# The last six blocks' up-projections by Strassen's seven block products, with weight sums made by GpSimd

## What is computed

```python
def _L1_cond_ref(x, t_emb, router_W, router_bias, w1, w3, w2, W1e, W2e):
    ...
    shared = jax.nn.silu(xf @ w1) * (xf @ w3) @ w2
    s = jax.nn.sigmoid((jnp.concatenate([xf, tf], axis=-1) @ router_W).astype(jnp.float32))
    ...
    h = jax.nn.gelu(jnp.einsum('nc,ech->enh', xf, W1e), approximate=False)
    y = jnp.einsum('enh,ehc->enc', h, W2e)
    routed = jnp.einsum('ne,enc->nc', combine, y)
    return ((shared + routed) / (N_SHARED + K)).reshape(Bb, Tt, C)
```

## Time and profile before

| | us |
|---|---|
| median of 3 runs (range) | 1062.59 (1060.21 to 1063.48) |
| the profiled execution: its time | 1061.99 |
| the profiled execution: its span | 1060.3 |
| PE busy | 1047.2 (99%) |
| DVE busy | 500.5 (47%) |
| ACT busy | 380.1 (36%) |
| POOL busy | 144.9 (14%) |

### The profile page before, as it was taken

The page is one execution under the profiler, slowest core; times in us unless marked ns, Lnnn a source line. Parts: engine busy times, 40 slices in busy tenths (PEclk is TensorE's granted clock), DMA queues, the critical chain, the costliest instruction groups (busy, mean ns, idle before and its releaser), DMA issues.

```text
span 1060.3 us, 15124 instructions
## 1 busy us (share of the span) xinstructions
PE 1047.2 (99%) x5098; PEld 855.1 (81%) x5098; DVE 500.5 (47%) x1054; ACT 380.1 (36%) x655; POOL 144.9 (14%) x171
## 2 busy tenths in 40 slices
PE   8999999999999999999999999999999999999998
PEld 6677777887888888888888888788888888888887
DVE  3117646456235665566555663454434244342335
ACT  3213334331226665666566663312121121211211
POOL 2020465420000000000000000322200202003020
PEclk9999999999999999999999999999999999999999
DMA  9956796997326868886577654637303333033131
GB/s 317 381 210 171 248 352 245 292 292 233 84 47 196 263 208 228 247 268 207 162 198 230 200 160 119 199 120 235 113 11 79 119 79 119 0 79 119 40 119 40
DMA packets 149416, 186.20 MB, mean 176 GB/s; under 512 B 9262, under 2 KB 93230, under 8 KB 149350
## 3 DMA queue, kind: packets, MB, share of 16 engines
q1 hardware_dynamic: 138598, 151.13, 47.4%
q0 software_dynamic: 10784, 34.61, 9.8%
HBM read 118.09 MB, written 67.63 MB: 175 GB/s over the span
## 4 chain that ended last, share of the span: by engine, by line
PE 95%; DMA 2%; DVE 2%; issue 1%; ACT 0%; SPq 0%; ACTq 0%; DVEq 0%
PE K L1573 11%; PE K L1574 11%; PE K L1575 11%; PE M L1573 5%; PE M L1574 5%; PE L L1574 5%; PE Rb L1574 5%; PE M L1575 5%; PE Rb L1573 5%; PE L L1573 5%; PE Rb L1575 5%; PE L L1575 5%; PE M L1615 2%; PE M L1617 2%; PE M L1619 2%; PE Rb L1689 2%
## 5 line engine op out<-in xcount | busy, mean ns | idle before, releaser
L505 ACT ACTIVATE slf<-K 128x512 f32<-128x512 f32 x64 | 38.2, 598 | 204.6 <-PE K L1575 204.6
L510 ACT CAST gTh<-slf 128x512 fp32r<-128x512 f32 x64 | 39.8, 621 | 182.1 <-DVE slf L520 180.5
L1573 PE MATMUL M<-w2h,gTh 128*128 128x512 f32 x256 | 99.8, 390 | 0.5 <-DVE gTl L524 0.5
L1574 PE MATMUL M<-w2l,gTh 128*128 128x512 f32 x256 | 99.6, 389 | 0.0
L1575 PE MATMUL M<-w2h,gTl 128*128 128x512 f32 x256 | 99.6, 389 | 0.0
L844 POOL DMA_INDIRECT yb<-ys_d,pos_fix x64 | 61.8, 965 | 272.5 <-DVE total L1492 254.6
L1573 PE MATMUL K<-x1h,w13h 128*128 128x512 f32 x224 | 87.2, 389 | 1.5 <-ACT yo L999 1.5
L1575 PE MATMUL K<-x1h,w13l 128*128 128x512 f32 x224 | 87.1, 389 | 0.0
L1574 PE MATMUL K<-x1l,w13h 128*128 128x512 f32 x224 | 87.1, 389 | 0.0
L520 DVE TENSOR_TENSOR slf<-L,slf 128x512 f32<-128x512 f32 x32 | 22.1, 690 | 132.7 <-PE L L1575 128.1
L1419 DVE TENSOR_TENSOR e2l<-e2raw,e2h 128x512 fp32r<-128x512 f32 x64 | 41.3, 686 | 79.9 <-ACT e2h L978 79.9
(11 more groups left out here) (298 smaller groups left out, 2475.1 us busy)
## 6 DMA issues: line engine op xcount, KB each, us to landing
w2c<-in_L_cond_w_dram SPq DMA_DIRECT2D x8, 2048.0 KB, 11.5
e1raw<-in_L_cond_W1e_dram SPq DMA_DIRECT2D x16, 1024.0 KB, 7.1
e2raw<-in_L_cond_W2e_dram SPq DMA_DIRECT2D x16, 1024.0 KB, 5.5
xr<-xs_d SPq DMA_DIRECT2D x64, 256.0 KB, 4.6
ys_d<-yo SPq DMA_DIRECT2D x32, 512.0 KB, 7.4
x_d<-x1tok SPq DMA_DIRECT2D x9, 1024.0 KB, 6.1
xs_d<-zeros SPq DMA_DIRECT2D x8, 1024.0 KB, 8.4
xres<-x_d SPq DMA_DIRECT2D x8, 1024.0 KB, 5.8
```

Of the source, the lines that this page charges most:

```text
L505: nc.scalar.activation(slf[:, h % 2], U[h % 2][:], ACT.Silu).then_inc(ffn.silu, 1)
L510: nc.scalar.copy(gTh[:, h % 2], slf[:, h % 2]).then_inc(ffn.g_hi, 1)
L1573: mm(o, ah, bh_, start=start, stop=False)
L1574: mm(o, ah, bl_, start=False, stop=False)
```

## The change

Split the 512 channels into two halves A and B, and the 512 tokens of a block into two halves. For a chunk of 128 hidden columns, (w1, w3) by (A, B) is a 2 x 2 arrangement of blocks, and the tokens are another: eight block products of 128 hidden columns by 256 channels by 256 tokens. Strassen's scheme (in Winograd's form) makes seven products of sums and differences of blocks instead. In the last six blocks of tokens the 24 matmuls of 512 columns of a chunk become 7 x 2 x 3 = 42 matmuls of 256 columns.

What this needs:

- **Weights.** For each of the 8 chunks seven weight blocks (four loaded, three of them made, plus one sum that is only a step), each cut in high and low: `wide`, 1792 + 1792 elements in each partition. POOL makes them before its first gather, for all 8 chunks in turn. Six chunks of them go out to DRAM (`wide_d`) and are loaded again in every block by transfers issued on ACT (`load_wide`, 128x3584 float32, 1.8 MB); two chunks stay in SBUF. PE and DVE begin the six blocks only when POOL is through (`WIDE_DONE`).
- **Tokens.** Four mixes of 128x512 on DVE for each block (`mix_x`), and seven casts and seven cuts (`cut_x1`) instead of four.
- **Products.** Each of the seven lands in half a bank (`place`). DVE joins them into U and V: seven additions of 128x256 for a chunk (`mix`), each with one input in PSUM, most waiting for the one before. ACT copies the first product to `m1s`. Silu now reads SBUF, in place, and the multiplication has both inputs in SBUF.
- **Order.** The silu, multiplication and cuts of a chunk stand behind the products of the next one; PE makes the down-projection of the chunk before in two parts, after the sixth and the seventh product.

```diff
+            wide = [sb(f"wide{i}", [P, 2, NP, 2, P], F32R, st) for i in range(4)]
+            parts = sb("parts", [P, 8, 2, P], F32, st)
...
+            cuts = [sb(f"cuts{i}", [P, 2, NP, 2, P], F32, st) for i in range(4)]
...
+        def place(i):
+            return G[i // 2][:, i % 2 * HT:i % 2 * HT + HT]
+        def home_of(h):
+            return {0: 0, 4: 1, 1: 2, 5: 2, 2: 3, 6: 3, 3: 4, 7: 4}[h]
...
+                n_p[0] += 1
+                ins.then_inc(consts, 1)
+                pool.wait_ge(consts, n_p[0])
+            pool.wait_ge(raw_in, RAW_0)
+            pool.wait_ge(S.v_ps, 2 * HC)
+            stored = {}
+            for i, h in enumerate((3, 5, 6, 7, 1, 2, 0, 4)):
+                alone(pool)
+                for at_, w, k in ((UP1_A, w1, 0), (UP1_B, w1, 1), (UP3_A, w3, 0), (UP3_B, w3, 1)):
+                    pool.dma_start(parts[:, at_], w.rearrange("(k p) c -> p k c", p=P)[:, 2 * k:2 * k + 2, h * P:(h + 1) * P]
+                                   ).then_inc(raw_in, 16)
+                pool.wait_ge(raw_in, RAW_0 + 64 * (i + 1))
+                for to, a, b, op in ((SUM_1, UP3_A, UP3_B, ALU.add), (SUM_2, SUM_1, UP1_A, ALU.subtract),
+                                     (DIF_3, UP1_A, UP3_A, ALU.subtract), (DIF_4, UP1_B, SUM_2, ALU.subtract)):
+                    link(nc.gpsimd.tensor_tensor(parts[:, to], parts[:, a], parts[:, b], op))
+                slot = {0: 0, 4: 1}.get(h, 2 + i % 2)
+                if slot in stored:
+                    pool.wait_ge(wide_out, WIDE_0 + 16 * stored[slot])
+                hi, lo, all_ = wide[slot][:, 0], wide[slot][:, 1], parts[:, 0:NP]
+                big, less = cuts[slot][:, 0], cuts[slot][:, 1]
+                link(nc.gpsimd.tensor_scalar(big, all_, SPLIT, None, ALU.mult))
+                link(nc.gpsimd.tensor_tensor(less, big, all_, ALU.subtract))
+                link(nc.gpsimd.tensor_tensor(hi, big, less, ALU.subtract))
+                link(nc.gpsimd.tensor_tensor(lo, all_, hi.bitcast(F32), ALU.subtract))
+                if h in STREAMED:
+                    alone(pool)
+                    pool.dma_start(wide_d[STREAMED.index(h)], wide[slot][:].rearrange("p a i k c -> p (a i k c)").bitcast(F32)
+                                   ).then_inc(wide_out, 16)
+                    stored[slot] = len(stored) + 1 if slot not in stored else max(stored.values()) + 1
+            assert n_p[0] == WIDE_DONE
...
-            def cut_x1(b):
-                for c in range(KC):
-                    nc.scalar.copy(x1h[:, c], x1raw[:, c].rearrange("p t n -> p (t n)")).then_inc(xf_hi, 1)
+            def cut_x1(b, i, free=True):
+                hi, _, of, made = XM[i]
+                act.wait_ge(xq_turned, b * MADE + made)
+                if free:
+                    act.wait_ge(prod_ps, b * (NP * HC) + (i + 1 - NP))
+                nc.scalar.copy(hi, of).then_inc(xf_hi, 1)
...
+                alone(act)
+                act.dma_start(wide[home_of(h)][:].rearrange("p a i k c -> p (a i k c)").bitcast(F32), wide_d[STREAMED.index(h)]
+                              ).then_inc(wide_in[home_of(h) - 2], 16)
...
+            def end_gate(b, h):
+                act.wait_ge(mixed, b * (MIXES * HC) + (MIXES * h + MIXES))
+                nc.scalar.activation(slf[:, h % 2], slf[:, h % 2], ACT.Silu).then_inc(F.silu, 1)
...
+            def fblock(b, ends):
+                for h in range(HC):
+                    none = first(b) and h == 0
+                    was = (b, h - 1) if h > 0 else (b - 1, HC - 1)
+                    if not none:
+                        end_gate(*was)
+                        if was[1] in (1, 2, 3):
+                            load_wide(was[1] + 4)
+                        if was[1] in (5, 6, 7) and not (ends and h > 0):
+                            load_wide(was[1] - 4)
+                    act.wait_ge(prod_ps, b * (NP * HC) + (NP * h + 2))
+                    nc.scalar.copy(m1s[:], place(0)).then_inc(m1_sb, 1)
+                    if not none:
+                        split_gate(*was)
+                    if h == 0 and not first(b):
+                        cut_x1(b, NP - 1)
+                    if h == HC - 1 and not ends:
+                        for i in range(NP - 1):
+                            cut_x1(b + 1, i)
+            fblock(0, False)
+            with act.Fori(1, NF - 1) as b:
+                fblock(b, False)
+            fblock(NF - 1, True)
+            end_gate(NF - 1, HC - 1)
+            split_gate(NF - 1, HC - 1)
...
+            def mix_x(b, i):
+                dve.wait_ge(xq_turned, b * MADE + (TT + i))
+                to, a, c = ((xsum[:, 0], raw(0, 1), raw(0, 0)), (xsum[:, 1], raw(1, 1), xsum[:, 0]),
+                            (raw(0, 1), raw(1, 1), raw(0, 1)), (xdif[:], raw(1, 0), xsum[:, 1]))[i]
+                tt(to, a, c, ALU.subtract).then_inc(xq_turned, 1)
+            def cut_x1(b, i):
+                hi, lo, of, _ = XM[i]
+                dve.wait_ge(xf_hi, b * NP + (i + 1))
+                tt(lo, of, hi.bitcast(F32), ALU.subtract).then_inc(xf_lo, 1)
...
+            def mix(b, h, i, to, other):
+                dve.wait_ge(prod_ps, b * (NP * HC) + (NP * h + min(i // 2 * 2 + 2, NP)))
+                tt(to, place(i), other, ALU.add).then_inc(mixed, 1)
+            def end_gate(b, h):
+                dve.wait_ge(mixed, b * (MIXES * HC) + (MIXES * h + 4))
+                mix(b, h, 6, slf[:, h % 2, HT:T], slf[:, h % 2, HT:T])
+            def by_silu(b, h):
+                dve.wait_ge(F.silu, b * HC + (h + 1))
+                tt(slf[:, h % 2], vv[:, h % 2], slf[:, h % 2], ALU.mult).then_inc(F.g_f, 1)
...
+            def fblock(b, work):
+                for h in range(HC):
+                    none = first(b) and h == 0
+                    was = (b, h - 1) if h > 0 else (b - 1, HC - 1)
+                    s1, s2 = slf[:, h % 2, 0:HT], slf[:, h % 2, HT:T]
+                    v1, v2 = vv[:, h % 2, 0:HT], vv[:, h % 2, HT:T]
+                    todo = work.get(h, {})
+                    if not none:
+                        end_gate(*was)
+                    todo.get("first", lambda: None)()
+                    if not none:
+                        by_silu(*was)
+                    todo.get("second", lambda: None)()
+                    if not none:
+                        split_gate(*was)
+                    dve.wait_ge(m1_sb, b * HC + (h + 1))
+                    mix(b, h, 1, s2, m1s[:])
+                    dve.wait_ge(mixed, b * (MIXES * HC) + (MIXES * h + 1))
+                    mix(b, h, 2, v1, s2)
+                    dve.wait_ge(mixed, b * (MIXES * HC) + (MIXES * h + 2))
+                    mix(b, h, 3, v2, v1)
+                    mix(b, h, 3, s2, s2)
+                    todo.get("third", lambda: None)()
+                    mix(b, h, 4, s1, m1s[:])
+                    dve.wait_ge(mixed, b * (MIXES * HC) + (MIXES * h + 3))
+                    mix(b, h, 5, v1, v1)
+                    todo.get("last", lambda: None)()
+            def split_gate(b, h):
+                dve.wait_ge(F.g_hi, b * HC + (h + 1))
+                tt(gTl[:, h % 2], slf[:, h % 2], gTh[:, h % 2].bitcast(F32), ALU.subtract).then_inc(F.g_lo, 1)
...
+            for t in range(TT):
+                turn_tile(0, t)
+            dve.wait_ge(consts, WIDE_DONE)
+            mix_x(0, 0)
+            cut_x1(0, 0)
+            mix_x(0, 1)
+            cut_x1(0, 1)
+            mix_x(0, 2)
+            for i in (2, 3, 4):
+                cut_x1(0, i)
+            mix_x(0, 3)
+            for i in (5, 6):
+                cut_x1(0, i)
+            prepare(KEPT, 0)
+            start_sum(0, range(TT))
...
+            def head(b):
+                return {0: {"first": all_of((cut_x1, b, 4)), "second": all_of((cut_x1, b, 5)), "third": all_of((cut_x1, b, 6)),
+                            "last": all_of((prepare, b + (F0 - 1), b + 1), (start_sum, b + 1, (0, 1)))},
+                        1: {"second": all_of((start_sum, b + 1, (2,))), "third": all_of((start_sum, b + 1, (3,)))}}
...
+                fblock(b, {**head(b),
+                           **{h: {"third": all_of((turn_tile, b + 1, h - 2)), "last": all_of(*ends[2 * h - 4:2 * h - 2])}
+                              for h in range(2, 6)},
+                           6: {"third": all_of((mix_x, b + 1, 0), (mix_x, b + 1, 1)),
+                               "last": all_of((mix_x, b + 1, 2), (mix_x, b + 1, 3))},
+                           7: {"third": all_of((cut_x1, b + 1, 0), (cut_x1, b + 1, 1)),
+                               "last": all_of((cut_x1, b + 1, 2), (cut_x1, b + 1, 3))}})
...
+            def down(b, h, ts_):
+                pe.wait_ge(F.g_lo, b * HC + (h + 1))
+                for t in ts_:
+                    if h == 0:
+                        pe.wait_ge(acc, t + 1 if first(b) else acc_before(b + 1) + (t + 1))
+                    rows, s_ = slice(t * P, (t + 1) * P), h % 2
```

(22 more changed lines are left out.)

188 lines of the change are left out of this document (124 added, 64 removed).

## The result

The changed kernel takes **1196.5 us** (median of 4, 1194.2 to 1196.9) against 1062.3 for the kernel before on the same chip: ratio 1.127, 95% interval 1.1255 to 1.1282, 134 us slower. Forecast were 1088 (1047 to 1110): the sign was right, the size far off. The profiled execution has a span of 1192.4 us, 132 more than before.

What follows compares the result with a forecast made beforehand. PE was taken to bound the kernel (busy 95% of the chain that ended last). From the profiled 1062 us, 10 gained in the six blocks and 36 lost in the experts' stage gave 1088 us, own range 1066 to 1112, stated 1047 to 1110.

Steps and rivals of the forecast that it cites:

- the length of POOL's chunk: Experts' stage: POOL's arithmetic, loads and the cuts let in between take 24.3 to 29.6 us for each of 8 chunks.
- the lead set against it: Experts' stage: the cuts' lead of some us over PE is used up first, lowering the loss from 41 to 36 us.
- hidden: the reloads: Six blocks: six 1.8 MB weight loads per block, issued three chunks (22.8 us) ahead, cost PE no time.
- the turn put at 0.62 us: Six blocks, chunks 2 to 5: DVE's turn of rows costs 0.62 us, with two sums 1.96 us, within the free 2.0.
- I take it as the same lock, held for a whole instruction: Experts' stage: DVE's cuts with two SBUF inputs wait for POOL's whole instruction, as POOL does for theirs; 20 to 62 us lost.
- the middle of 20 and 62, less a lead: Experts' stage: loss taken as the middle, 41 us, less the cuts' lead over PE, giving 36 us.
- Products: Six blocks: 2016 matmuls of 256 columns at 0.116 us replace 1152 of 512 at 0.2268, 27.4 us less.
- 0.0135 remains fixed: PE's pace: if 0.0135 us per matmul doesn't scale with columns, 256 columns take 0.1202 us, saving 19.0 us.
- the weight-bound row of 64 columns: PE's pace: 64 columns with full 128x128 weights need 0.116 us, set by the weight load; taken for 256 columns.
- What the blocks give back: Six blocks: four losses of 4, 4, 6.5 and 3 us, 17.5 together (12 to 24), leave a gain of 10.
- Hand-over: Between experts' stage and six blocks: seven casts and the mixes ahead of yo delay PE's first product by 6.5 us.
- Rival 1: Experts' stage: DVE does not wait for POOL, the stage stays at 348 us, time 1052 (1045 to 1059); chance 0.30.

Runs made afterwards that it cites:

- e1: The changed kernel with GpSimd's 64 arithmetic operations replaced by memsets of the same tiles, weight sums left out: 1125.6 us, ratio 1.058 to the kernel before.
- e3: The changed kernel with each of GpSimd's 1792-element operations made as seven of 256 elements: 1124.8 us, ratio 1.060 to the kernel before.
- e2: The changed kernel with the next block's xq loaded first, ahead of SyncE's wait for the started sums and the load of xres: 1156.2 us, ratio 1.089.
- e4: The changed kernel without its 34 reloads of wide in the six blocks, chunks using other chunks' weights: 1165.9 us, ratio 1.098 to the kernel before.
- e12: The changed kernel without GpSimd's weight loads, sums, stores and the reloads; xq first, ScalarE's rows between casts, first block's sums later: 1116.8 us, ratio 1.020 (third chip).
- e5: The changed kernel with ScalarE's four yo copies put between its casts for the first block instead of behind all seven: 1233.4 us, ratio 1.129 (second chip).
- e6: The changed kernel with xq loaded first, GpSimd's operations in pieces of 256 and ScalarE's rows between its casts: 1125.0 us, ratio 1.033 (second chip).

## Why the prediction was wrong, step by step

Two steps failed: the length of POOL's chunk and the lead set against it (46 of the 107 us missed), and "hidden: the reloads", together with the turn put at 0.62 us (38). Both mechanisms of the miss are shown by runs that take them away, e1 and e3 for the one, e2 for the other.

- **"I take it as the same lock, held for a whole instruction": right, in both directions.** The Trainium skill's rule (SBUF — State Buffer, Who interferes with whom) agrees: cuts are held up to 4.5 us by operations that read, and by memsets not at all. Also right: one group's worth of cuts passes in one POOL chunk, and the loss falls on PE's `mm1` and `mm2`.
- **The sum of POOL's chunk was mis-sized**, 24.3 to 29.6 us for 33.1. The multiplication cost 4.85 us, not 2.9; the differences 4.2 to 4.35 (bounds 2.9 to 4.4, my middle too low), a sum 0.94, not 0.5 to 0.7: arithmetic of 21.5 us a chunk, not 13.6 to 18.9. POOL waited 46.3/8 = 5.8 us for the parts to land (6.9 in a chunk in the middle), where I had put 2.7. Against that, the 5.5 us for DVE's cuts between POOL's instructions are not there: POOL's next one starts 0.08 us behind the last (396.54, 396.62), while the cut is still at work. By the prediction's own rule: 33.1 - 21.8 = 11.3 us, 8 times, is 90; measured 82, forecast 36. The step "the middle of 20 and 62, less a lead" took comfort from DVE's idle time. Idle time is a mean over the stage, and the measured loss of 82 is nearly the 90 of the rule without any lead. 46 us of the miss.
- **"Hidden: the reloads" failed, though they were never waited for.** The prediction asked only when PE would wait for `wide`. It didn't ask what 180 GB/s more do to the others on the queues: `xq` 7.3 to 11.9 us, the first `yb` to 12.5. And it costed the move of the turn from chunk 4 to chunk 2 at its 0.62 us without looking when its rows are issued (SyncE, behind `acc` and `xres`). e2 prices this at 38 us of the 51 that the blocks lost (e4, without the traffic, at 30: the two overlap). It is the largest part of what turned a gain of 10 in the blocks into a loss of 51, though not all of it: e2's blocks are still 13 us longer than before.
- **Products**: 0.120 us apart, the upper of the three readings ("0.0135 remains fixed"), not 0.116; the weight-bound row of 64 columns was the wrong neighbour. And a matmul of 512 came 0.232 apart, not 0.2268. A chunk: 42 x 0.120 + 12 x 0.232 = 7.82 instead of 7.59, 11 us in 48 chunks. The Trainium skill's gap (TensorE: Matmul & The Clock Gate, Back-to-back issue gap), an estimate of 0.109, is further off.
- **What the blocks give back**: with 7.82 us a chunk the products save 16 us, not 27.4. e2's blocks are 13 longer than before, so 30 us of overheads stand there where 17.5 were priced (bounds 12 to 24): 12 us of the miss. They are not in the steady blocks (62.8 us, 0.3 above PE's 8 x 7.82) but in the first and the last. Some are the waits behind the first `yb` (4.2 and 1.5 us) and the half clock behind the longer ones; the rest was not taken apart. The prediction's "2 to 14 gained" was also narrower than its own terms, which allow 19.0 - 24, a loss of 5.
- **Hand-over**: forecast 6.5 us more than before; PE was idle for 7.5 where it was 1.5, 6.0 more. Right. Not priced: behind it the products are 0.21 us apart until 755, half clock, and behind the wait of 4.3 us for `vv` at 932 the granted clock was 0.66 for 10 us.
- **Rival 1**, that DVE does not wait for POOL, had 0.30 and is excluded by one timeline row. Even then the forecast of 1052 would have failed: without any hold, e1 is 5.8% slower.

What adds up, in us of the profiled executions: stage +82, blocks +51, less 1 ahead of the stage, together the 132 of the spans. Against the forecast of 36 lost and 10 gained the miss is 46 in the stage and 61 in the blocks: 38 the late `xq`, 11 the pace, 12 the overheads.

What stays open: whether e12's edit would gain on the first chip, where a steady block falls to 62.8 us. From e2's blocks there, an estimate: 13 us above before, which are 10 won in four steady blocks, 17 lost in the first and 7 in the last; e5's edit gives some 4 of these back, and without the reloads the 6 us of waits behind `yb` go too. That leaves some 4 us lost, but was not run there.

## What to carry to other kernels

Work put on an idle GpSimd is not free if VectorE reads two SBUF operands at that time: make GpSimd's instructions short (e3: 1 us instead of 4.2 to 4.85) before counting on idle time. Before a transfer is called hidden, look at who else lands by the same queues, and when a step is moved earlier, find the instruction that issues its input. A scheme that saves 2.4 us of 65 in a steady block has to repay its first and last block out of that: count these before the saving.

## What the runs showed of the hardware, unexpected

- The hold works with a one-operand GpSimd read too (copy of 1792: 2.0 us, longest cut 2.17), and not with a memset (1.60 us, cuts 0.67 to 0.69). Behind the multiplication by a constant the cut is let go early: one of 3.91 us that starts at 350.03 inside L908 (349.65, 5.05 us) ends 0.76 us ahead of it.
- GpSimd at float32, 1792 elements, beside a working VectorE: memset 1.60, copy 2.0, difference 4.2 to 4.35, multiplication by a constant 4.85 us. In pieces of 256: 1.01 to 1.06 us each in e3 (0.96 to 1.12 in e6), 7.2 instead of 4.3 us for the same 1792.
- Three chips needed 1062, 1093 and 1094 us for the kernel before, 3% apart, and on two of them PE pauses for about 0.5 us once a block; the products may be worth 2.4 us a block on the one chip (e2) and nothing on another (e12).
